# Four column groups for the attention values, and denominators from sums that GpSimd makes

## The reference, cut to what matters

```python
scores = jnp.einsum('bhsd,bhtd->bhst', q, k) * scale
attn = jax.nn.softmax(scores, axis=-1)
o = jnp.einsum('bhst,bhtd->bhsd', attn, v_c)
...
return o @ W_O + b_O
```

## Time and profile before

| | us |
|---|---|
| median of 3 runs | 1046.83 (1044.38 to 1052.82) |
| profiled execution | 1046.84, span 1045.0 |
| first attention, first score of the second pass to last `values` | 55.5 to 363.0 |
| one full unit | 39.75 |
| PE busy in the span | 904.0 (87%) |
| DVE / ACT / POOL busy in the span | 596.0 / 505.8 / 148.0 |

### The profile page before, as it was taken

The page is one execution under the profiler, slowest core; times in us unless marked ns, Lnnn a source line. Parts: engine busy times, 40 slices in busy tenths (PEclk is TensorE's granted clock), DMA queues, the critical chain, the costliest instruction groups (busy, mean ns, idle before and its releaser), DMA issues.

```text
span 1045.0 us, 15144 instructions
## 1 busy us (share of the span) xinstructions
PE 904.0 (87%) x5002; PEld 523.4 (50%) x5002; DVE 596.0 (57%) x1338; ACT 505.8 (48%) x855; POOL 148.0 (14%) x205
## 2 busy tenths in 40 slices
PE   5899999999999986859949754599999999999858
PEld 2343443444443373549948633356555555565445
DVE  6876776866874055523316639575765755756051
ACT  3335455455455543216625421256665575665632
POOL 4300000000000052450050281101011011000000
PEclk9889999999999996879989956689999999999969
DMA  8200000000000000111221210000000000000001
GB/s 313 116 0 1 1 1 1 1 0 0 0 1 1 1 1 15 49 48 41 77 61 39 70 40 0 1 1 2 1 1 1 2 0 0 0 1 2 1 1 41
DMA packets 22629, 24.31 MB, mean 23 GB/s; under 512 B 3591, under 2 KB 20105, under 8 KB 22314
## 3 DMA queue, kind: packets, MB, share of 16 engines
q1 hardware_dynamic: 19896, 17.90, 5.3%
q0 software_dynamic: 2048, 4.20, 1.3%
q10 hardware_dynamic: 626, 1.43, 0.4%
HBM read 14.34 MB, written 9.18 MB: 23 GB/s over the span
## 4 chain that ended last, share of the span: by engine, by line
PE 69%; DVE 16%; issue 6%; ACT 5%; another core or an unknown queue 3%; DMA 1%; POOL 0%; DVEq 0%; ACTq 0%; SPq 0%; POOLq 0%
PE ps L983 12%; PE ps L1306 8%; PE ps L951 7%; PE ps L972 6%; PE ps L1358 5%; PE ps L1332 4%; DVE mx_part L1981 4%; PE ps L1249 3%; PE ps L934 2%; ACT rounded L552 2%; ACT pt L798 2%; PE ps L1159 2%; PE ps L1310 2%; PE ps L1231 1%
## 5 line engine op out<-in xcount | busy, mean ns | idle before, releaser
L607 ACT ACTIVATE pt<-ps 128x512 f32<-128x512 f32 x256 | 139.6, 595 | 110.6 <-PE ps L972 110.0
L798 ACT ACTIVATE pt<-ps 128x1024 f32<-128x1024 f32 (+1 forms) x160 | 142.7, 937 | 88.4 <-PE ps L1332 45.8
L1600 DVE TENSOR_REDUCE mx_part<-ps 128x1 f32<-128x512 f32 x256 | 161.8, 684 | 30.7 <-PE ps L951 29.8
L1981 DVE TENSOR_REDUCE mx_part<-ps 128x1 f32<-128x512 f32 (+3 forms) x256 | 138.9, 585 | 37.0 <-PE ps L1310 24.2
L1306 PE MATMUL ps<-rounded 128*128 128x512 f32 (+3 forms) x384 | 144.2, 427 | 16.0 <-issue 5.4
L983 PE MATMUL ps<-pt,ckv_cur 128*33 128x512 f32 x512 | 135.6, 608 | 0.0
L552 ACT ACTIVATE rounded<-ps 32x512 fp32r<-32x512 f32 (+2 forms) x134 | 79.5, 593 | 109.1 <-PE ps L934 35.4
L951 PE MATMUL ps<-rounded 98*128 98x512 f32 x256 | 112.6, 452 | 3.0 <-DVE rounded L1584 1.8
L1306 PEld LDWEIGHTS ps<-rounded 128*128 128x128 f32 x384 | 73.8, 203 | 81.2 <-DVE mx_part L1981 49.2
L1332 PE MATMUL ps<-rounded 128*128 128x512 f32 (+3 forms) x384 | 105.3, 374 | 8.9 <-ACT pt L798 7.2
L1981 DVE TENSOR_REDUCE mx<-ps 128x1 f32<-128x128 f32 (+3 forms) x128 | 57.1, 487 | 92.8 <-PE ps L1310 79.3
(11 more groups left out here) (255 smaller groups left out, 1186.2 us busy)
## 6 DMA issues: line engine op xcount, KB each, us to landing
wm<-in_wm SPq DMA_DIRECT2D x1, 4896.0 KB, 15.3
kstage<-to_experts SPq DMA_DIRECT2D x10, 256.0 KB
of_experts<-pt SPq DMA_DIRECT2D x10, 256.0 KB, 3.1
to_experts<-kstage SPq DMA_DIRECT2D x4, 512.0 KB, 4.1
wm<-in_experts SPq DMA_DIRECT2D x1, 1028.0 KB
x<-in_x SPq DMA_DIRECT2D x4, 256.0 KB, 5.8
out<-x SPq DMA_DIRECT2D x4, 256.0 KB, 2.3
to_experts<-kstage SPq DMA_DIRECT2D x2, 448.0 KB, 5.3
```

The source lines that it names most:

```text
L607: nc.scalar.activation(pt[:, (HP * t + h) % 8, :], ps[:, ST0_BANKS[h], :], ACT.Exp, scale=SCALE0).then_inc(exp_done, 1)
L798: nc.scalar.activation(pt[:, 4 * (t % 2) + 2 * g:4 * (t % 2) + 2 * g + 2, 0:w], ps[:, ST1_BANKS[2 * g]:ST1_BANKS[2 * g] + 2, 0:w], ACT.Exp ...
L1600: v.tensor_reduce(mx_part[pp][:, s:s + 1], ps[:, banks[s % len(banks)], :], AX_X, ALU.max).then_inc(max_done, 1)
L1981: v.tensor_reduce(dst, ps[:, banks[s % len(banks)], o:o + w], AX_X, ALU.max).then_inc(max1_done, 1)
```

## The change: what it does

A step is now one key tile `k` for two heads and both query halves, so a unit has 8 steps of four `scores`, four exponentials and one `values` of four products, each 32 columns wide, at rows 0, 32, 64 and 96 of bank 6. The column of ones is gone. POOL adds the exponentials of two key tiles (`pair_adds`, 16 additions a unit) and then those pairs (8 more), 128 x 512 each. PE multiplies the sums of four key tiles by a 128 x 32 block of ones into bank 3, twice a unit (`denominators`), so that each denominator already stands on the 32 rows of its context. DVE takes a reciprocal of 128 x 512 and two products of 64 x 512 into `ctxT`, which is already laid out for the output product. The transposes of the contexts (L992, L1102) go.

The maxima are made up to two units ahead: nine pieces of unit 1 before unit 0 starts, 12 pieces of unit u+2 in steps 5 to 7 and the other 20 of unit u+1 in steps 0 to 4. `cq` is used directly for the first pass, and POOL copies it to `query_stack` twice per batch instead of DVE twice per unit. `vo` and the bias (now 128 rows) are made before unit 0, and POOL adds the bias to x in unit 0. The units are all written out.

```diff
+MX0 = [(h, j, c) for c in range(QH) for h in range(HP) for j in range(TS)]
...
+    here = [(0, 4), (1, 2), (2, 5), (3, 5), (4, 4)] if u else [(0, 5), (1, 4), (2, 5), (3, 5), (4, 4)]
...
+MAX0_AHEAD = 9
+Z0_AT = {0: (1, 2), 1: (1, 3), 3: (2, 0), 4: (2, 1)}
+TURN0_AT = {(5, 1): 0, (6, 0): 1, (6, 1): 2, (7, 0): 3}
+DEN0_AT = {6: 0}
...
+            def pair_adds(u, j):
+                G = u * NPAIR + j
+                if G and j % 2 == 0:
+                    pool.wait_ge(quad_add, G // 2 * HQ)
+                for i in range(HQ):
+                    pool.wait_ge(exp_done, (u * TS + 2 * j + 1) * HQ + i + 1)
+                    if i == 0 and j % 2 and G >= 2:
+                        pool.wait_ge(den_mm, G // 2)
+                    nc.gpsimd.tensor_tensor(pair_sum[j % 2][i], pt0(0, i), pt0(1, i), ALU.add).then_inc(pair_add, 1)
+                if j % 2:
+                    for i in range(HQ):
+                        pool.wait_ge(pair_add, (G - 1) * HQ + HQ + i + 1)
+                        nc.gpsimd.tensor_tensor(pair_sum[1][i], pair_sum[0][i], pair_sum[1][i], ALU.add).then_inc(quad_add, 1)
...
+            def exp0(u, pp, k, i):
+                G = u * TS + k
+                act.wait_ge(st_mm, G * HQ + i + 1)
+                if G >= 2 and i == 0:
+                    act.wait_ge(pv_mm, G - 1)
+                if G >= 2 and k % 2 == 0:
+                    act.wait_ge(pair_add, (G // 2 - 1) * HQ + i + 1)
+                nc.scalar.activation(pt0(k, i), ps[:, ST0_BANKS[i % 2], :], ACT.Exp, scale=SCALE0).then_inc(exp_done, 1)
...
+                for i in range(HQ):
+                    ins = mm(ps[ctx_rows(pp, i), CTX_BANK, :], ckv[:, k, u // UH, :], pt0(k, i), start=(k == 0), stop=(k == TS - 1))
...
+            def denominators(u, pp, j):
+                if j == 0 and u:
+                    pe.wait_ge(ctx_out, 3 * (u - 1) + 1)
+                pe.wait_ge(quad_add, (u * NDEN + j + 1) * HQ)
+                for i in range(HQ):
+                    ins = mm(ps[ctx_rows(pp, i), DEN_BANK, :], ones[:, 0:DC], pair_sum[1][i], start=(j == 0), stop=(j == NDEN - 1))
...
+            def contexts_out(u):
+                pp, b, g = u % 2, u // UH, u % UH // 2
+                dve.wait_ge(den_mm, (u + 1) * NDEN)
...
+                v.reciprocal(cT[:, 0, :], ps[:, DEN_BANK, :]).then_inc(ctx_out, 1)
...
+                    v.tensor_tensor(ctxT[rows, b, g, c, :], cT[rows, 1, :], cT[rows, 0, :], ALU.mult).then_inc(ctx_out, 1)
...
-                    ins = mm(o, ones[0:1, :], vo_bias[:], start=False, stop=True)
+                        ins = mm(o, ctxT[:, b, g, cc, t * P:(t + 1) * P], vo[:, cc, g, :], start=(g == 0), stop=(g == 1))
...
+            o_mms(0)
+            denominators(U0 - 1, 1, NDEN - 1)
+            for c in range(1, NCH):
+                o_mms(c)
```

More of the change, by code:

```diff
@@ new lines, in _ @@
+            pool.wait_ge(prep_done, 6)
+            pool.wait_ge(ln_xn, NT)
+            pool.wait_ge(ln_turn, NCH)
+            for u in range(U0):
+                for j in range(NPAIR):
+                    pair_adds(u, j)
+                    if u == 0:
+                        xc = x[:, j * TC:(j + 1) * TC, :]
+                        nc.gpsimd.tensor_tensor(xc, xc, vo_bias[:].unsqueeze(1).broadcast_to([P, TC, D]),
+                                                ALU.add).then_inc(bias_add, 1)
+                    if u in (UH - 1, UH) and j < QH:
+                        if j == 0:
+                            pool.wait_ge(st_mm, u * TS * HQ)
+                        copy_cq((u + 1) % 2, 1, j)
@@ new lines, in unit0, with piece, turn @@
+            def unit0(u, pp):
+                slots = max_slots(u)
+                def piece(k, n):
+                    if slots[k][n]:
+                        scores_max(*slots[k][n])
+                def turn(k, end):
+                    if u + 1 < U0 and (k, end) in TURN0_AT:
+                        turn_max(u + 1, TURN0_AT[k, end])
+                for k in range(TS):
+                    for i in range(2):
+                        scores(u, pp, k, i)
+                        piece(k, i)
+                    if k:
+                        values(u, pp, k - 1)
+                    elif u:
+                        values(u - 1, 1 - pp, TS - 1)
+                    if k == 2 and u:
+                        denominators(u - 1, 1 - pp, NDEN - 1)
+                    if k in DEN0_AT:
+                        denominators(u, pp, DEN0_AT[k])
+                    turn(k, 0)
+                    for i in range(2, HQ):
+                        scores(u, pp, k, i)
+                        piece(k, i)
+                    piece(k, 4)
+                    if k in Z0_AT:
+                        du, n = Z0_AT[k]
+                        if u + du < U0:
+                            make_z(u + du, n, None if n == 2 else 4 * (u + du) + n)
+                    turn(k, 1)
@@ L1040, in _ @@
             first_cq(1)
-            for n in range(len(MX0)):
-                scores_max(0, 0, n, True)
+            for n in range(NMX0):
+                scores_max(0, n)
                 if n == 2:
@@ L1673, in _ @@
             z_lo_part(0, 0, 1)
-            for n in range(len(MX0)):
-                maximum(0, 0, n, True)
+            for n in range(NMX0):
+                maximum(0, n)
                 if n == 1:
```

506 lines of the change are left out of this document (218 added, 288 removed).

## The result

| | before | changed | forecast |
|---|---|---|---|
| median, us | 1045.61 (1042.71 to 1052.82, 4 runs) | **1065.77** (1064.26 to 1067.03, 4 runs) | 1046 |
| profiled execution, span | 1046.84, 1045.0 | 1067.03, 1065.1 | |

The account below looks back on a forecast made before the run. PE alone was taken to set the pace. From the profiled 1046.84 us, unit 1's start (-2.4), units 1 to 5 (-4.8), unit 6 (-2.7) and the end (+9.0) gave -0.9: 1046 us, range 1020 to 1066.

Parts of the forecast that it names:

- POOL, with four additions of the bias more (5.1), holds unit 1's step 2 by 1.2: 34.8: Unit 0: PE's 30.1 us, 3.5 for half clock and POOL's delay of 1.2 make it last 34.8 us.
- the other edits: Before and in unit 0: 6 us more work ahead, unit 0 starts at 61.5, unit 1 at 96.3, 2.4 earlier.
- the lump: DVE's reciprocal and two products between the maxima of steps 2 and 3, about 6.0 us with waits beside POOL.
- the clock term: Each full unit: the idle stretch brings PE's clock down; 3.4 us of work at half clock, 1.7 lost, 38.8 a unit.
- PE's list: PE's own work in a full unit, falling from 39.75 to 31.5 us.
- the lump's stretch: PE idle in step 3, waiting for a bank: 5.6 us a unit; with 31.5 of work, 37.1 before the clock.
- Full work resumes at once: After each idle stretch in a full unit: the reason for taking 3.4 us at half clock, below the 10.1 bound.
- rival 3: Full units: PE stays at half clock for 10.1 us of work, 3.4 a unit more, +20, 1066 us; chance 0.20.
- The end: Unit 7's start to PE's next work behind the norm: POOL and DVE make it 61.8 against 52.7 us, +9.0.
- POOL's loop: Exponentials of an even step wait for the previous pair's additions: 16.6 us per four steps, 33.2 a unit.
- rivals 1 and 2: Full units: products unhindered or clock up, or both, 1024 (taken as 1026), chance 0.20; shorter reciprocal, 1012, chance 0.10.
- rival 2: Full units: reciprocal of 0.69 us, POOL then the bound at 33.2 a unit, six units -34, 1012 us; chance 0.10.

Follow-up runs that it names:

- p: Changed kernel with split_max's maximum made as a reduction into PSUM bank 3, where its other instructions read it: 1014.56 us, ratio 1.009 to the kernel before.
- g: Changed kernel with each of POOL's additions in unit 0 waiting for the end of the one before: 1021.62 us, ratio 1.015 to the kernel before.
- l: Changed kernel with 20 unused products in PE's idle stretch of step 3, units 2 to 6: 1014.33 us, ratio 1.008 to the kernel before.
- r: Changed kernel with units 0 to 6 divided on 8 of 512 columns only, and split_max through PSUM: 984.65 us, ratio 0.980 to the kernel before.
- m: Changed kernel with the division of units 0 to 6 made on 8 of 512 columns only: 1022.15 us, ratio 1.015 to the kernel before.
- d: Changed kernel with a copy in place of the reciprocal, so the division is left out: 1016.96 us, ratio 1.010 to the kernel before.
- f: Changed kernel with 14 unused products in PE's idle stretch of step 3, units 2 to 6: 1027.65 us, ratio 1.022 to the kernel before.
- c: Changed kernel with the reciprocal written in place in PSUM, so the products have one input there: 1013.72 us, ratio 1.007 to the kernel before.
- b: Changed kernel with split_max's first instruction, a maximum of two SBUF inputs, written as a reduction of one input: 1023.14 us (one run).
- n: Changed kernel with POOL's pauses in unit 0, the reciprocal in place in PSUM, and unit 7's denominators by PE alone: 1002.65 us, ratio 0.995 to the kernel before.

## Why the prediction was wrong

**The step that failed: "POOL, with four additions of the bias more (5.1), holds unit 1's step 2 by 1.2: 34.8"**, in the part on the other edits. It counted POOL's additions as time on POOL's own list, and within the units only the lump's two products were charged with a wait beside POOL. `split_max`, three DVE instructions with their inputs in SBUF, beside the longest run of POOL in the kernel, was charged nothing. It cost 10.9 of the 12.6 that unit 0 was off (p); it waited 9.83 us, to the end of POOL's run, and with pauses in that run 1.07 (g).

**Mis-sized: the clock term.** The mechanism was right: an idle stretch in every unit, then 0.50. Where I took 3.4 us of work at half clock, 1.7 lost, it was 7.1 of work and 3.0 lost (l). Units 2 to 5 were 2.1 each over the forecast, 8.3 of the +8.8 together. 1.3 of each is the clock. The other 0.8 is what l has over the 37.1 that I had without the clock: PE's list 0.7 longer and some 1.1 of short waits that I had not priced, less 0.9 of the lump's stretch that I had too long. "Full work resumes at once" was no reason for a shorter stretch: unit 0's start had been low for 10.1 us, and the lumps of units 3 to 5 are followed by 10.2, those of units 2 and 6 by 6.8. That row was the nearest one, and rival 3 took it, but it charged 10.1 us of *work* at half clock; 3 us of the low stretch are idle. Unit 1's 38.4 against 38.8 is luck: PE's stretch there was 1.0 and not 5.6, and what filled the rest no run isolates.

**Rival 3** gave 1066, which is the time measured, but by luck: of its +20 for the clock some 5 came (1.3 in each of units 2 to 5), and 11 from `split_max`.

**Right.** Four products side by side: 1.06 against 1.05. POOL's addition: 1.25 to 1.29 (1.27). PE's list: 32.2 (31.5). The reciprocal: 3.35 (3.0), the two products 3.26 (2.9 with their waits), the lump 6.6 (6.0). PE's idle stretch: 4.71 (5.3, and 0.3 for the next piece). The end: 60.85 (61.8), with the second addition to x 49.2 after unit 7's start (50.2) and PE's next work 11.6 later (11.6). Unit 0's start: 63.53 (61.5, bounds 58.5 to 64.5), though it moves by 4.4 between executions. Periods without the lump: 32.6 to 33.7, near the 33.2 of POOL's loop and near PE's 32.2 as well.

**What the sum could not show:** rivals 1 and 2 priced a shorter lump at 22 and 34 us. With `split_max` out of POOL's way rival 2's price is near: from p to r, side by side, it is 29.9, though in r the filling of `ctxT` makes unit 1 longer than in p (42.0 for 38.4). With `split_max` as it was, m won 6. Each cause hid what the other was worth. Rival 2's own condition, a reciprocal of 0.69, was not met (3.35), and d, which put a copy of 0.68 in its place, won 12 and not 34.

## What to carry to other kernels

Before work moves to POOL, list every DVE instruction whose operands all lie in SBUF and that will run beside it, however small. Charge each with one POOL instruction, and take the rest of POOL's run as the upper bound; or give it an input in PSUM. An idle stretch of PE costs more than itself: here 4.7 us idle cost 3.0 more in clock. Filling all but 1.5 of it gained nothing (f), and filling it whole gained all (l); shortening it to 2.9 with less DVE work gave back half of the 3.0 (c). When taking away a cost gains little, look what moved into its place before calling the cost small.

## What the hardware showed

- POOL and DVE: with POOL's instructions back to back (starts 1.22 us apart, 1.27 each) a DVE instruction of 16 elements lasted 9.83 (the changed kernel), 9.65 (b) or 5.83 us (m), to the end of POOL's run. With a pause of 0.14 us behind each POOL instruction it took 1.07 (g). The Trainium skill (SBUF — State Buffer, section "Summary: rules for kernel authors") says, of a DVE instruction with two SBUF inputs and a GpSimd one that reads SBUF, that the second one to issue "fully blocks until the first finishes"; in this case the trace agrees for the products of the lump, 1.6 each, and shows more for `split_max`: it blocks through up to eight instructions.
- Neither the size of the DVE instruction nor the missing pause decides it alone. In the norm POOL's five additions stand just as close (8.19 us for five of 1.67), and an instruction of 128x8 got in after one of them (1.58), as did the four `TENSOR_SCALAR` of 128x128 that follow beside POOL, at some 1.7 each. In r the two products of 64x8 take 2.31 together beside POOL's additions in unit 1. Why these get in after one and `split_max` does not is open.
- A reduction from SBUF to SBUF (0.19 in b) and the instructions with an input in PSUM (0.19 in p, 0.70 in c) did not wait beside the same POOL work; a `TENSOR_SCALAR` from SBUF to SBUF did (9.65 in b).
- A DVE reciprocal of 128x512 takes 3.35 us, of 128x8 0.204: some 6.2 ns an element, and as long in PSUM (3.36). The Trainium skill's repeat count of 8 (VectorE: DVE Perf Modes, section "First, the fixed hardware budget"), taken as eight cycles of 0.96 GHz an element, would make it 4.3, an estimate by that page; the measurement decides against it.
- The granted clock, once at 0.50, stayed there for 3.4 us (c, PE busy throughout), 6.8 (f, the same), 10.2 (the changed kernel, 7.1 of 10 busy) and 17.1 (n, 15.8 busy). I found no rule in these rows that tells which.
